# Latent attention, two heads at a time: one rotated query tile per head instead of one shared by both

## What is computed

```python
q_hk   = (hidden_q @ Wq.T).reshape(B, S, H, 128)
q_big  = einsum('bshk,hkq->bshq', q_hk, w_kc_q)          # 192 wide per head
q_big  = q_big * cos_q + rotate_half(q_big) * sin_q
kv_r   = kv_c * cos_k + rotate_half(kv_c) * sin_k        # 64 wide
q_r    = einsum('bshq,hqr->bhsr', q_big, W_qr)           # r = 64
k_r    = einsum('bld,hdr->bhlr', kv_r, W_kr)
scores = einsum('bhsr,bhlr->bhsl', q_r, k_r)
ctx_c  = einsum('bhsl,bld->bhsd', softmax(scores), kv_r)
out    = (w_kc_kv per head, then Wo) applied to ctx_c
```

## Time and profile before

| what | value |
|---|---|
| median of 3 runs (lowest, highest) | 867.09 us (865.51, 869.0) |
| profiled execution, its own time | 868.19 us |
| its span, first to last instruction | 866.4 us |
| mean granted TensorE clock | 0.930 |
| busy share of the span: TensorE matmul, VectorE, ScalarE, GpSimd | 86%, 65%, 50%, 24% |
| stretch of the latent attention's pairs | about 137 to 452 us |

### The profile page before, as it was taken

One profiled execution on the slowest core, in us unless ns is written; L12 is line 12 of the kernel. 1 busy time (PEld: TensorE's weight loads), 2 busy tenths in 40 slices (PEclk: granted clock), 3 DMA queues, 4 the chain that ended last, 5 costly groups with the idle time before them and its releaser, 6 DMA issues. The chain is left out here.

```text
span 866.4 us, 13304 instructions
## 1 busy us (share of the span) xinstructions
PE 744.5 (86%) x4826; PEld 479.7 (55%) x4826; DVE 560.8 (65%) x1081; ACT 430.5 (50%) x894; POOL 203.6 (24%) x300
## 2 busy tenths in 40 slices
PE   6999958998989999898876368999859999849998
PEld 3455646665666666665552253666533444438887
DVE  5568666655656565755648872566477999674866
ACT  4547732636354453636348755455255666623332
POOL 2413020113030303213043712231022111261440
PEclk9989998999999999999997786999957999958999
DMA  4615412201111120210014204130020233402111
GB/s 126 169 41 158 145 33 69 72 26 49 28 45 40 34 72 1 72 28 14 13 27 134 56 9 132 52 112 3 1 56 7 60 73 84 126 2 75 73 49 48
DMA packets 49759, 52.23 MB, mean 60 GB/s; under 512 B 10116, under 2 KB 40388, under 8 KB 49588
## 3 DMA queue, kind: packets, MB, share of 16 engines
q1 hardware_dynamic: 45718, 50.37, 21.0%
q10 hardware_dynamic: 3978, 1.02, 0.5%
HBM read 26.58 MB, written 2.04 MB: 33 GB/s over the span
## 5 line engine op out<-in xcount | busy, mean ns | idle before, releaser
L522 DVE TENSOR_REDUCE a_nm<-ps 128x2 f32<-128x512 f32 (+1 forms) x112 | 75.5, 689 | 33.1 <-PE ps L824 19.8
L2512 DVE TENSOR_REDUCE x_nm<-ps 128x2 f32<-128x512 f32 x128 | 85.0, 687 | 12.7 <-PE ps L2653 10.5
L2597 ACT ACTIVATE x_pt<-ps 128x1024 f32<-128x1024 f32 x64 | 62.5, 1021 | 35.0 <-PE ps L2681 34.3
L1446 ACT ACTIVATE m_junk<-ps,m_nm 128x256 bf16<-128x256 f32 x128 | 58.6, 484 | 36.7 <-DVE m_nm L1309 36.7
L1283 DVE TENSOR_TENSOR m_qcs<-ps,mw_tab 128x512 f32<-128x512 f32 x96 | 61.8, 686 | 22.1 <-PE ps L1569 21.2
L1569 PE MATMUL ps<-m_xp,m_mp 128*128 128x512 f32 x288 | 74.4, 399 | 1.6 <-DVE m_wr L1297 1.6
L1269 POOL TENSOR_SCALAR fw<-fw,finv 128x256 f32<-128x256 f32 x24 | 11.6, 481 | 255.5 <-PE ps L1649 255.5
L2653 PE MATMUL ps<-kx,a_qs 96*128 96x256 bf16 x256 | 53.3, 297 | 8.2 <-DMA a_qs<-a_ks 6.5
L1569 PEld LDWEIGHTS ps<-m_xp,m_mp 128*128 128x128 f32 x288 | 51.9, 190 | 13.7 <-issue 4.5
L3028 PE MATMUL ps<-x_xp,x_wp 128*128 128x512 f32 x216 | 54.9, 405 | 0.0
L3028 PEld LDWEIGHTS ps<-x_xp,x_wp 128*128 128x128 f32 x216 | 40.7, 194 | 8.7
(11 more groups left out here) (302 smaller groups left out, 1726.2 us busy)
## 6 DMA issues: line engine op xcount, KB each, us to landing
a_qs<-a_parts SPq DMA_DIRECT2D x48, 128.0 KB
a_ks<-a_parts SPq DMA_DIRECT2D x48, 128.0 KB
m_q<-m_qs SPq DMA_DIRECT2D x32, 128.0 KB
x_gb<-scr_g SPq DMA_DIRECT2D x8, 512.0 KB, 3.8
fw<-in_f_w SPq DMA_DIRECT2D x12, 256.0 KB
a_qs<-a_ks SPq DMA_DIRECT2D x48, 64.0 KB
mw_wq<-in_m_wq SPq DMA_DIRECT2D x8, 256.0 KB, 2.8
mw_wo<-in_m_wo SPq DMA_DIRECT2D x8, 256.0 KB, 2.9
```

The costliest lines, as they stand in the source:

```text
L522: dve.tensor_reduce(dst, src, AX.X, ALU.max, negate=True).then_inc(mx_done.sem, 1)
L1446: act.activation(junk[:, n % 4, :], c.ps[:, S_BANKS[k % 4], qt * SEQ:(qt + 1) * SEQ], ACT.Exp, bias=nm[:, k // 4, one], accum_out=den[:, k ...
L2512: dve.tensor_reduce(nm[:, n % ITEMS, QT * u:QT * u + QT], c.ps[:, u % 2, :].rearrange("p (t k) -> p t k", t=QT), AX.X, ALU.max, negate=Tru ...
L2597: act.activation(pt[:, n % 2, kt, :], c.ps[:, 2 + 2 * kt:4 + 2 * kt, :].rearrange("p b n -> p (b n)"), ACT.Exp, scale=SCALE).then_inc(exp_ ...
```

## The change

- `rotate` of the shared tile 1 writes one tile per head instead of one for cosine and one for sine: `qcs[:, half, 1, h, :]` holds the 64 dimensions of head h times cosine in one half of the partitions and times sine in the other. That takes four VectorE instructions of 64 x 512 in place of two of 128 x 512; two of them write to the other half of the partitions.
- `scored_shared` replaces `scored_both`: two calls as before, but one per head, each with a weight 64 columns wide and written to that head's 64 partitions.
- `wr` keeps 64 columns per tile, in slots (first or second part) x tile; for tile 1 the part is the head. `absorb` writes 64 columns per call, all six in one bank, with one head's half of `wkrT`; `absorbed_weights` is one copy of 128 x 384 instead of two.
- `turned_weights` lays `wrT` out as six tiles, so that a tile-1 weight holds the cosine and the sine dimensions of one head; still five copies.
- The counts of the waits follow (`rotated`), and `shift_transpose` of the second half no longer waits for `wr_done`. The DMAs and the inputs stay as they are.

```diff
-        wrT, wkrT = sb("wrT", [P, 2, 3, P]), sb("wkrT", [P, 2 * CTX])
-        wr = sb("wr", [P, 2, 2, 3, 2 * R])
+        wrT, wkrT = sb("wrT", [P, 6, P]), sb("wkrT", [P, 2 * CTX])
+        wr = sb("wr", [P, 2, 2, 3, R])
...
+        WR_SLOTS = ((0, 2), (1, 4), (5, 3))
...
+        def rotated(p, k):
+            return 16 * p + 8 * (k // 3) + (0, 4, 6)[k % 3]
...
                 def rotate(p, k):
                     half, tile = k // 3, TILE_ORDER[k % 3]
                     dve.wait_ge(qb.sem, 6 * p + k + 1)
+                    if tile == 1:
+                        for h in range(2):
+                            for cs in range(2):
+                                dve.tensor_tensor(
+                                    qcs[rows((cs, 1 - cs)[h]), half, 1, h, :].rearrange("p (b q) -> p b q", q=SEQ),
+                                    c.ps[rows(h), QB_BANKS[k], :].rearrange("p (b q) -> p b q", q=SEQ),
+                                    tab[rows(h), cs, 1, :].unsqueeze(1).broadcast_to([R, 2, SEQ]), ALU.mult)\
+                                    .then_inc(rope.sem, 1)
+                        return
...
                 def absorbed_weights(p, bank):
-                    for cs in range(2):
-                        dve.wait_ge(absorbed.sem, 2 * p + cs + 1)
-                        dve.tensor_scalar(wr[:, p % 2, cs, :, :].rearrange("p t n -> p (t n)"),
-                                          c.ps[:, bank + cs, 0:3 * P], 1.0, None, ALU.mult).then_inc(wr_done.sem, 1)
+                    dve.wait_ge(absorbed.sem, p + 1)
+                    dve.tensor_scalar(wr[:, p % 2, :, :, :].rearrange("p j t n -> p (j t n)"),
+                                      c.ps[:, bank, 0:6 * R], 1.0, None, ALU.mult).then_inc(wr_done.sem, 1)
...
-                    act.activation(wrT[:, 0, :, :].rearrange("p t n -> p (t n)"), ps[:, 0:3 * P], ACT.Copy)\
+                    dst = wrT[:, :, :].rearrange("p t n -> p (t n)")
+                    act.activation(dst.rearrange("p (k n) -> p k n", n=DCQ)[:, 0:4:3, :],
+                                   ps[:, 0:2 * DCQ].rearrange("p (h n) -> p h n", h=2), ACT.Copy)\
                         .then_inc(turned_ev.sem, 1)
-                    for s in range(2):
-                        act.activation(dst[:, :, s, :], src[:, :, 1 - s, :], ACT.Copy).then_inc(turned_ev.sem, 1)
+                    act.activation(dst[:, DCQ:DCQ + 448].rearrange("p (h n) -> p h n", h=2)[:, :, 0:160],
+                                   ps[:, 32:352].rearrange("p (h n) -> p h n", h=2), ACT.Copy).then_inc(turned_ev.sem, 1)
+                    act.activation(dst[:, 352:416].rearrange("p (h n) -> p h n", h=2),
+                                   ps[:, 0:2 * DCQ].rearrange("p (k n) -> p k n", n=32)[:, 0:12:11, :], ACT.Copy)\
+                        .then_inc(turned_ev.sem, 1)
...
-                    for cs in range(2):
+                    for j in range(2):
                         for tile in range(3):
-                            mm = pe.matmul(c.ps[:, bank + cs, tile * P:(tile + 1) * P], wrT[:, cs, tile, :], wkrT[:, :],
+                            h = (0, j, 1)[tile]
+                            mm = pe.matmul(c.ps[:, bank, (3 * j + tile) * R:(3 * j + tile + 1) * R],
+                                           wrT[:, WR_SLOTS[tile][j], :], wkrT[:, rows(h)],
                                            start=True, stop=True)
-                        mm.then_inc(absorbed.sem, 1)
+                    mm.then_inc(absorbed.sem, 1)
...
-                def scored_both(p, half):
-                    pe.wait_ge(rope.sem, 12 * p + 6 * half + 2)
+                def scored_shared(p, half):
+                    pe.wait_ge(rope.sem, rotated(p, 3 * half + 1))
...
-                    for cs in range(2):
-                        pe.matmul(c.ps[:, 4 + half, :], wr[:, p % 2, cs, 1, :], qcs[:, half, 1, cs, :],
-                                  start=(cs == 0), stop=False, skip_group_check=True)
+                    for h in range(2):
+                        pe.matmul(c.ps[rows(h), 4 + half, :], wr[:, p % 2, h, 1, :], qcs[:, half, 1, h, :],
+                                  start=True, stop=False, skip_group_check=True)
...
                 def scored_own(p, half):
-                            mm = pe.matmul(c.ps[rows(h), 4 + half, :], wr[:, p % 2, cs, tile, rows(h)],
+                            mm = pe.matmul(c.ps[rows(h), 4 + half, :], wr[:, p % 2, cs, tile, :],
...
                 def shift_transpose(p, half):
-                    elif p + 1 < PAIRS:
-                        pe.wait_ge(wr_done.sem, 2 * p + 4)
-                    else:
+                    elif p + 1 == PAIRS:
                         pe.wait_ge(added.sem, 4 * p)
```

More of the change, by code:

```diff
@@ L1417, in turned_weights @@
                     ps = c.ps[:, TURN_BANK, :]
-                    src = ps[:, 0:3 * P].rearrange("p (h s n) -> p h s n", h=2, s=2)
-                    dst = wrT[:, 1, :, :].rearrange("p t n -> p (t n)").rearrange("p (h s n) -> p h s n", h=2, s=2)
-                    act.activation(wrT[:, 0, :, :].rearrange("p t n -> p (t n)"), ps[:, 0:3 * P], ACT.Copy)\
+                    dst = wrT[:, :, :].rearrange("p t n -> p (t n)")
+                    act.activation(dst.rearrange("p (k n) -> p k n", n=DCQ)[:, 0:4:3, :],
+                                   ps[:, 0:2 * DCQ].rearrange("p (h n) -> p h n", h=2), ACT.Copy)\
                         .then_inc(turned_ev.sem, 1)
-                    for s in range(2):
-                        act.activation(dst[:, :, s, :], src[:, :, 1 - s, :], ACT.Copy).then_inc(turned_ev.sem, 1)
+                    act.activation(dst[:, DCQ:DCQ + 448].rearrange("p (h n) -> p h n", h=2)[:, :, 0:160],
[3 more added lines that the diff above has]
+                        .then_inc(turned_ev.sem, 1)
                     for h in range(2):
@@ L1559, in packed @@
                             pe.wait_ge(xp_lo.sem, xp_lo.at(4))
-                            pe.wait_ge(wr_done.sem, 2)
+                            pe.wait_ge(wr_done.sem, 1)
                     if k < 2 and p:
@@ L1565, in packed @@
                     if k >= 4:
-                        pe.wait_ge(rope.sem, 12 * p + 2 * (k - 3))
+                        pe.wait_ge(rope.sem, rotated(p, k - 3))
                     terms = [(dt, w, x) for dt in range(DT) for w, x in TERMS3]
@@ L1572, in packed @@
                     mm.then_inc(qb.sem, 1)
-                def scored_both(p, half):
-                    pe.wait_ge(rope.sem, 12 * p + 6 * half + 2)
+                def scored_shared(p, half):
+                    pe.wait_ge(rope.sem, rotated(p, 3 * half + 1))
                     if half == 0:
-                        pe.wait_ge(wr_done.sem, 2 * p + 2)
+                        pe.wait_ge(wr_done.sem, p + 1)
                         if p:
@@ L1581, in scored_both @@
                         pe.wait_ge(wn_lo.sem, wn_lo.at(p + 1))
-                    for cs in range(2):
-                        pe.matmul(c.ps[:, 4 + half, :], wr[:, p % 2, cs, 1, :], qcs[:, half, 1, cs, :],
-                                  start=(cs == 0), stop=False, skip_group_check=True)
+                    for h in range(2):
+                        pe.matmul(c.ps[rows(h), 4 + half, :], wr[:, p % 2, h, 1, :], qcs[:, half, 1, h, :],
+                                  start=True, stop=False, skip_group_check=True)
                 def scored_own(p, half):
-                    pe.wait_ge(rope.sem, 12 * p + 6 * half + 6)
+                    pe.wait_ge(rope.sem, rotated(p, 3 * half + 3))
                     for cs in range(2):
                         for h, tile in ((0, 0), (1, 2)):
-                            mm = pe.matmul(c.ps[rows(h), 4 + half, :], wr[:, p % 2, cs, tile, rows(h)],
+                            mm = pe.matmul(c.ps[rows(h), 4 + half, :], wr[:, p % 2, cs, tile, :],
                                            qcs[:, half, tile, cs, :], start=False, stop=(cs == 1),
@@ L1599, in scores @@
                     if k < 4:
-                        pe.wait_ge(rope.sem, 12 * p + 6 + 2 * k)
+                        pe.wait_ge(rope.sem, rotated(p, 3 + k))
                     else:
@@ L1655, in product @@
                         if p + 1 < PAIRS:
-                            pe.wait_ge(wr_done.sem, 2 * p + 4)
+                            pe.wait_ge(wr_done.sem, p + 2)
                         else:
@@ L1713, in _ @@
                     packed(p, 3)
-                    scored_both(p, 0)
+                    scored_shared(p, 0)
                     if p:
@@ L1724, in _ @@
                         fold(p + 1)
-                    scored_both(p, 1)
+                    scored_shared(p, 1)
                     for k in range(4):
```

## The result

The changed kernel took 857.08 us (median of 4 runs, 854.19 to 860.75), the kernel before beside it 867.89. The ratio is 0.9886, with a 95% interval of 0.9843 to 0.9929: 1.1% faster. The profiled execution of the changed kernel took 854.19.

The account below looks back on a forecast made before the run. A pair was taken as a relay of TensorE, VectorE and ScalarE, where only earlier maxima count. Seven pairs at 1.36 (9.5), 0.56 for the last and 0.47 before the first made 10.5 us: 856.6, range 851.5 to 863.5.

Parts of the forecast that it names:

- The shared product: On TensorE, twice a pair: two narrow calls overlap and take 1.06 us instead of 1.62, saving 0.56 each.
- The first maximum: On VectorE in seven pairs: starts 0.89 us earlier, 0.56 from its own chain plus 0.33 of slack.
- the slack behind `fold_rest`: VectorE's 0.39 us idle before the first maximum, waiting for scores; about 0.33 of it counted as recoverable.
- my 0.23: Part of TensorE's saving per pair, in us, expected to become idle time before the shifts' transpose instead of gain.
- The copy: Folded weights copied on VectorE by one instruction instead of two: second maxima 0.47 us earlier in seven pairs.
- The preparation and the first pair: Before the first pair one weight-copy instruction goes, 0.47 us; the pair's first maximum gains 0.89.
- The last pair's first maximum: Not among the maxima that wait for scores; it follows VectorE's own chain and gains only 0.56 us.
- `absorb` and the added rotations: Nothing either way: narrower TensorE matmuls save nothing counted; VectorE's extra 2.74 us a pair is hidden.
- The pieces of cover: VectorE idle times, 1.14 and 1.59 us before adds and 1.15 before `context_rest`, expected to hide the added rotations.
- The clock: Expected at 1.00 in pairs 1 to 6; rival: idler TensorE drops to 1.2 GHz, time 868.5 us, chance 0.06.
- The price of 1.7 us: Upper cost of one clock drop, read from the last pair's 3.4 us at 1.2 GHz; seven pairs: 11.9 us.
- A stage behind this one: Stages after latent attention were expected to keep their length; a change there would count against the prediction.

Follow-up runs that it names:

- `wide_first`: Changed kernel with only the first half's shared product wide again (128-column weights, 128 partitions): 859.72 us, ratio 0.992.
- `wide_second`: Changed kernel with only the second half's shared product wide again (128-column weights, 128 partitions): 858.91 us, ratio 0.9908.
- `two_copies`: Changed kernel with the copy of the folded weights made twice, the first into an unused tile: 861.82 us, ratio 0.991.
- `filled`: Changed kernel plus an unused matmul call in TensorE's idle time before the transpose of the shifts (two longer in the last pair): 857.73 us, ratio 0.9879.
- `two_rotations`: Changed kernel with two 128-partition rotations for the shared tile in place of four of 64: 860.14 us, ratio 0.9911.
- `more_k3`: Changed kernel with four more unused 64 x 512 products ahead of the shared tile's second rotation: 866.61 us, ratio 0.9992.
- `more_k0`: Changed kernel with four more unused 64 x 512 products ahead of the shared tile's first rotation: 862.82 us, ratio 0.9954.
- `moved_copy`: Changed kernel with the copy of the folded weights moved behind the second four maxima: 857.19 us, ratio 0.989.

## Why the prediction was right

The forecast was 856.6 in a range of 851.5 to 863.5; 857.1 was measured. That the two are only 0.5 apart is luck, since four runs spread over 6.6 us; the stage's own gain, 11.1 against 10.5, is what the prediction can be held to, and most of its steps came out. By these steps:

- *The shared product* was to save 0.56 by timing it against L1590 and L1629; it saves 0.52 (1.62 to 1.10). The two narrow calls do overlap, and the entry into the narrow form costs 0.09, as read.
- *The first maximum* was to gain 0.89 in seven pairs. It gained 1.00. The term that was mis-sized is the slack behind `fold_rest`: I took 0.33 of the 0.39; the maximum starts 0.46 closer to it than before (1.34 to 0.88), since one instruction starts before the former has ended. With that, VectorE's chain (0.51) and slack (0.46) make 0.97, and TensorE's two savings (1.04) arrive at the same time. `wide_first` and `wide_second` show both halves worth 0.51. Nothing is clipped, against my 0.23.
- *The copy* was to give 0.47 in seven pairs; it gives 0.47 in the trace and 0.50 by `two_copies`.
- *The preparation and the first pair* were to give 0.47 + 0.89; they gave 1.42.
- *The last pair's first maximum* was to gain 0.56, and with the copy's 0.47 the period before it 1.03. That period, pair 6, ends 0.78 shorter (36.75 to 35.97). The reason is the clock: it stood at 0.95 in that stretch, behind the idle 0.73 and 0.53. With 1.00 the same pair takes 35.56 in `filled` and 35.58 in `two_rotations`, which would be 1.2 shorter. So the term itself was too small, 0.7 instead of 0.56, and a dip of 0.4 took more than the excess away.
- *`absorb` and the added rotations* at nothing: 1.55 against 1.60, and `two_rotations` makes no difference. The pieces of cover that I named, 1.14 and 1.59 before the adds and 1.15 before `context_rest`, are the ones that `more_k3` and `more_k0` use up.
- *The clock*: idle time before the transpose of the shifts went from 0.66 to 0.73 only (0.9 was forecast: the 0.23 that was to become idle time came through as gain). The prediction's sign was a clock of 1.00 in pairs 1 to 6; pairs 0 to 5 kept it, pair 6 did not, so this sign failed once. The chance of 0.06 was low: dips in pairs 0 to 5 appear in every variant of the changed kernel but the filled ones and `two_rotations`. The price of 1.7 us for each was too high, though: they cost up to 0.8, and nothing in the last pair, from which the 1.7 was taken.
- *A stage behind this one* was not to change its length. The code behind took 0.4 us more, and scatters by 6.7 over the executions shown.

The sum was 10.5, the stage gave 11.1. That the profiled execution is 14 us shorter and not 11 comes from the 3.4 us ahead of the stage.

The Trainium skill's rule that changing the tiling mode drains TensorE (TensorEngine Tiling (Array Packing), section Key Properties) agrees with the 0.09 and 0.10 of the two kernels; against 0.6 saved in the product itself it didn't decide. The skill's page TensorE: Matmul & The Clock Gate (section HAM oscillation) says that thin matmul work with gaps makes the clock fall back; `moved_copy` with and without the filler agrees in kind. The page's case is a wait for DMA longer than the matmul work ahead of it; here gaps of 0.75 and 0.53 in a pair of 37 us were enough, so that its case alone would not have foretold this.

## What to carry to other kernels

Where engines relay each other, find for each hand-over which side arrives last and by how much; a saving is worth what it moves at the next hand-over, and work added in front of a wait costs nothing until that wait is used up, here after another 1.6 to 1.8 us. Before making a helper step cheaper, try to move it behind the work that the other engine is waiting for: one call moved in the kernel before gave half of this change's gain. When TensorE gets thinner, read the granted clock pair by pair, the last ones too; a matmul of 0.76 us that nobody reads, put into the gap, saved 0.8 in each pair of the moved-copy kernel that had lost its clock, and 0.4 in pair 6 of the changed one. And where the code ahead of the change and behind it varies by nearly as much as the change brings, compare the change's stage alone, and pair by pair.

## What was unexpected of the hardware

A pair with a dip of the clock is up to 0.8 us longer than one without; in `two_copies` one pair with a dip was no longer at all. Gaps of 0.75 and 0.53 us, with all of TensorE's work around them, were followed by some 3.3 us at 1.2 GHz in four of seven pairs of one execution and in three of seven of another, the same pairs but for one, while the changed kernel with 0.73 and 0.53 had it in one of seven. With the filler of 0.76 us and no other change, seven of seven pairs kept 2.4 GHz. And the stretch ahead of the stage, the same code in all, reached the same point between 115.9 and 123.9 us, with the granted clock between 40 and 80 us at 1.00 or at 0.91.
